# A decoder block on one Trainium2 core: first loads ahead of the semaphore counts, one buffer fill moved, and 40 matmuls whose results nobody reads

## The reference

```python
nx = _ln(x, ln1_scale, ln1_bias)
q, k, v = heads(nx @ W_qkv)
x = x + attend(q, k, v, causal) @ W_self_out
nx = _ln(x, ln2_scale, ln2_bias)
q = heads(nx @ W_q)
k, v = heads(encoder_output @ W_kv)
x = x + attend(q, k, v, None) @ W_cross_out
nx = _ln(x, ln3_scale, ln3_bias)
return x + relu(nx @ W1 + b1) @ W2 + b2
```

## Time and profile before

| | us |
|---|---|
| median of 3 runs | 992.72 |
| lowest and highest | 990.99, 992.97 |
| the profiled execution, its own time | 988.45 |
| its span, first to last instruction | 986.7 |
| PE busy (share of the span) | 958.7 (97%) |
| VectorE busy | 742.7 (75%) |
| ScalarE busy | 639.8 (65%) |
| GpSimd busy | 257.2 (26%) |

### The profile page before, as it was taken

The page is one execution under the profiler, slowest core; times in us unless marked ns, Lnnn a source line. Parts: engine busy times, 40 slices in busy tenths (PEclk is TensorE's granted clock), DMA queues, the critical chain, the costliest instruction groups (busy, mean ns, idle before and its releaser), DMA issues.

```text
span 986.7 us, 20078 instructions
## 1 busy us (share of the span) xinstructions
PE 958.7 (97%) x7632; PEld 599.0 (61%) x7632; DVE 742.7 (75%) x1175; ACT 639.8 (65%) x1371; POOL 257.2 (26%) x451
## 2 busy tenths in 40 slices
PE   4999999999999999999999999999999999999998
PEld 3876665445545555445443764444444699999997
DVE  7579779999999999999923787888887844455542
ACT  4653357777778787777777324888888644444543
POOL 6522123333222223232244210111114312222210
PEclk9999999999999999999999998999999999999999
DMA  6996762232323131313525887334441111122001
GB/s 210 316 352 230 247 195 90 80 99 68 110 67 109 56 100 59 102 52 104 173 90 169 270 318 234 99 124 145 139 130 36 64 55 54 65 65 64 23 21 43
DMA packets 78272, 124.01 MB, mean 126 GB/s; under 512 B 10624, under 2 KB 51872, under 8 KB 73120
## 3 DMA queue, kind: packets, MB, share of 16 engines
q1 hardware_dynamic: 78176, 122.73, 38.1%
HBM read 72.48 MB, written 49.17 MB: 123 GB/s over the span
## 4 chain that ended last, share of the span: by engine, by line
PE 89%; DVE 7%; ACT 1%; DMA 1%; SPq 1%; issue 1%; POOL 0%; ACTq 0%; DVEq 0%
PE bank L862 20%; PE bank L841 17%; PE bank L717 12%; PE bank L698 10%; PE bank L699 9%; PE bank L700 9%; DVE mx L1222 6%; PE bank L896 3%; PE bank L690 3%; PE bank L725 2%; PE bank L685 2%; DMA xt<-in_x_dram 1%; PE bank L738 1%; ACT probs L1115 1%; DVE probs L1215 1%
## 5 line engine op out<-in xcount | busy, mean ns | idle before, releaser
L1115 ACT ACTIVATE probs<-bank 128x512 f32<-128x512 f32 (+3 forms) x1024 | 456.8, 520 | 113.7 <-PE bank L841 107.1
L1222 DVE TENSOR_REDUCE mx<-bank 128x2 f32<-128x1024 f32 (+5 forms) x416 | 435.6, 1084 | 32.8 <-PE bank L717 19.9
L841 PE MATMUL bank<-q_st,k_st 64*128 64x512 f32 (+3 forms) x1024 | 265.9, 425 | 4.8 <-ACT probs L1115 3.5
L862 PE MATMUL bank<-probs,nx_mem 128*32 128x512 f32 (+3 forms) x2048 | 230.8, 528 | 0.4 <-POOL probs L1583 0.4
L841 PEld LDWEIGHTS bank<-q_st,k_st 64*128 64x128 f32 x1024 | 131.4, 186 | 154.4 <-ACT probs L1115 138.8
L717 PE MATMUL bank<-k_st,q_st 62*128 62x154 f32 (+4 forms) x1280 | 217.8, 352 | 4.8 <-DVE mx L1222 2.1
L717 PEld LDWEIGHTS bank<-k_st,q_st 62*128 62x128 f32 x1280 | 131.0, 188 | 71.9 <-DVE mx L1222 54.9
L1583 POOL TENSOR_SCALAR_AFFINE_SELECT probs<-probs 128x256 f32<-128x256 f32 x256 | 103.7, 409 | 198.4 <-ACT probs L1115 196.2
L1592 POOL TENSOR_TENSOR oN<-oT,rs 128x256 f32<-128x256 f32 x64 | 40.6, 635 | 212.8 <-DVE rs L1326 212.8
L1153 ACT ACTIVATE hT<-bank,b_sb 128x512 f32<-128x512 f32 x64 | 44.2, 690 | 72.7 <-PE bank L700 72.7
L1474 DVE TENSOR_TENSOR hT_lo<-hT,hT_hi 128x512 fp32r<-128x512 f32 x64 | 42.7, 687 | 54.5 <-ACT hT_hi L1156 53.5
(11 more groups left out here) (126 smaller groups left out, 1263.7 us busy)
## 6 DMA issues: line engine op xcount, KB each, us to landing
q_st<-q_parts SPq DMA_DIRECT2D x48, 256.0 KB
q_st<-qx_parts SPq DMA_DIRECT2D x48, 256.0 KB
xt<-in_x_dram SPq DMA_DIRECT2D x16, 512.0 KB, 5.9
q_parts<-probs SPq DMA_DIRECT2D x16, 512.0 KB, 4.4
k_parts<-probs SPq DMA_DIRECT2D x16, 512.0 KB, 3.9
k_st<-k_parts SPq DMA_DIRECT2D x32, 256.0 KB
qx_parts<-probs SPq DMA_DIRECT2D x16, 512.0 KB, 4.8
v_aug<-vst_mem SPq DMA_DIRECT2D x8, 544.0 KB, 4.4
```

What stands on the lines that cost most here:

```text
L841: pe.matmul(bank[:, score_bank(a, use), 0:n], keys_of(a, v0)[rows, i // 2, P * kb:P * kb + P], q_st[w][rows, i // 2, lo:lo + n], start=Tru ...
L862: last = pe.matmul(bank[32 * i:32 * i + 32, acc_bank(a, v0, hf), lo - HF * hf:lo - HF * hf + n], v_cur[w // 2][:, col:col + 32], probs[:, ...
L1115: act.activation(probs[:, use % NPT, 0:n], bank[:, score_bank(a, use), 0:n], ACT.Exp, scale=SCALE).then_inc(a.exp_done, 1)
L1222: dve.tensor_reduce(mx[:, par, part].rearrange("p (j y) -> p j y", j=2)[:, :, blocks.start:blocks[-1] + 1:blocks.step], banks[:, :, 0:len( ...
```

## The change

Four edits.

1. SP issues the first loads (x, `wqkv`, the vectors, second x, `wkv`, `cx`) first and raises the 13 semaphores after them, ahead of `b2` and the three late weights.
2. VectorE's fill of `k_st[0]` moves from the start of its program to after the second normalization; that of `q_st[0]` stays. The counts that SP and ScalarE wait for follow (6 instead of 7 where the fill of `k_st[0]` isn't needed, 7 ahead of the first `load_stacks`).
3. At the beginning TensorE makes 18 fp32 matmuls of 128x128 by 128x128 of `ident` into bank 7 as soon as `ident` is there, and 8 more after the first transposes.
4. In the last self span it makes 3 fp32r matmuls (128x128 by 128x256, from pair 3 of the stacks, into the unused half of bank 5) at the end of step 13 and 3 at the end of step 14. In the halves 6 and 7 of `dense_c` it makes 4 (128x128 by 128x512, from `k_st[0]`, into bank 0) after the two tiles and ahead of the wait for `nxT`; the wait for `lo_ready` ahead of them is the one that stood before the first projection. Nobody reads what these 40 write.

```diff
-        def fill_stacks(eng, w, filled):
-            eng.memset(q_st[w][:, :, :].rearrange("p i t -> p (i t)").bitcast(F32), 0.0).then_inc(filled, 1)
-            eng.memset(k_st[w][:, :, :].rearrange("p i t -> p (i t)").bitcast(F32), 1.0).then_inc(filled, 1)
+        def fill_stacks(eng, w, filled, sides=(0, 1)):
+            for side in sides:
+                eng.memset((q_st, k_st)[side][w][:, :, :].rearrange("p i t -> p (i t)").bitcast(F32), float(side)).then_inc(filled, 1)
 ...
-            for s in range(8):
-                sp.sem_inc(A.parts_stored[s], 16)
-            for s in range(2):
-                sp.sem_inc(v_stored[s], 16)
-                sp.sem_inc(px_stored[s], 16)
-            sp.sem_inc(vx_stored, 16)
             load_x(A, x, 0, 0)
 ...
             load_ctx(0)
+            for s in range(8):
+                sp.sem_inc(A.parts_stored[s], 16)
+            for s in range(2):
+                sp.sem_inc(v_stored[s], 16)
+                sp.sem_inc(px_stored[s], 16)
+            sp.sem_inc(vx_stored, 16)
             sp.dma_start(b2_sb[:, :], b2.partition_broadcast(P)).then_inc(w_late, 16)
 ...
+            def keep_busy(dst, a, b, times):
+                for _ in range(times):
+                    pe.matmul(dst, a, b, start=True, stop=True)
+
             pe.wait_ge(consts_ok, 1)
+            keep_busy(bank[:, 7, 0:P], ident[:, :], ident[:, :], 18)
 ...
             transposes(A, 0, 0, 0)
+            keep_busy(bank[:, 7, 0:P], ident[:, :], ident[:, :], 8)
 ...
                 if step % 2 and step < 16:
                     project_c(0, step // 8, step // 4 % 2, (step // 2 % 2,))
+                if step in (13, 14):
+                    keep_busy(bank[:, 5, D:2 * D], k_st[3][:, 0, 0:P], q_st[3][:, 0, 0:D], 3)
 ...
                         between(i)
+                    if n >= LATE_X:
+                        pe.wait_ge(C.lo_ready, 2 + 2 * n - 1)
+                        keep_busy(bank[:, 0], k_st[0][:, 0, 0:P], k_st[0][:, 0, 0:HF], 4)
                     pe.wait_ge(C.nxT_ready, 2 * n + 2)
 ...
-            fill_stacks(dve, 0, ones_ok)
+            fill_stacks(dve, 0, ones_ok, (0,))
 ...
             normalize(A, xt, 1, 1)
+            fill_stacks(dve, 0, ones_ok, (1,))
             for b in range(B - 3):
                 dense_a(b, True)
```

More of the change, by code:

```diff
@@ L438, in _ @@
                 load_x(A, x, 1, hf)
-            sp.wait_ge(ones_ok, 7)
+            sp.wait_ge(ones_ok, 6)
             for b in range(B - 3):
@@ L486, in first_stacks @@
                         sp.wait_ge(A.parts_stored[s], 16 + 16)
-                    sp.wait_ge(ones_ok, 2)
+                    sp.wait_ge(ones_ok, 7)
                     load_stacks(SA, 0, 0)
@@ L1084, in _ @@
                                scale=lns_sb[:, 0, k:k + 1]).then_inc(nxT_high_a, 1)
-            act.wait_ge(ones_ok, 7)
+            act.wait_ge(ones_ok, 6)
             act.wait_ge(w_in, 16 * 6)
```

## The result

The changed kernel takes 997.33 us (median of 20 runs, 992.23 to 1000.07), the kernel before 990.3 in 20 runs on the same chips (988.09 to 992.97). The ratio is 1.0063, with a 95% interval of 1.005 to 1.0076: slower, by 0.63% or 6.2 us. That is the difference of the two means; the medians are 7.0 us apart. The forecast was +3.6 us.

A forecast was written before the change was run, and what follows sets the result against it. PE was taken to bound the kernel, busy 97% with the chain on it for 89%. Terms +1.0 + 0 + 0.7 + 1.9 + 0 = +3.6 us on 992.72 gave 996.3 us, range 990.5 to 998.8.

The forecast's parts named there:

- What it said would be seen: First load about 0.8, fill 18.5, moments 20.4, PE idle about 2 us, added matmuls without waits, slow stretches still there.
- The loads and the fill: At the beginning, loads free up to 0.8 us but the 1.76 us fill delays PE's third projection: +1.0, bounds -0.8, +1.8.
- The clock: Behind 530 and 609 us, work placed before dense stretches cannot fill the thin stretches behind: 0, bound -2.7.
- The 26 at the beginning: PE's start, where the chain stands on loads and VectorE, so a raised clock brings next to nothing: 0, -0.5 to +1.
- The 6 in the span: Last self span, 6 x 0.12 us between chain pieces without a gap: +0.7, from 0 to +1.4.
- the 8 in the halves: Halves 6 and 7, 4 x 0.235 us each behind the second tile, not hidden: +1.9, from 0 to +2.2.
- The clock was not held: Rival for stretches behind 530 and 609 us: added work prevents both slow stretches, -2.7 against +3.6, 993.6 us; chance 0.20.
- The faster case: Rival, whole change: added matmuls and fill hidden, loads pay fully, clock held, -3.5, 989.2 us; chance 0.13.
- Half hidden: Rival: fill absorbed behind PE, part of the halves' matmuls run while VectorE is late, about +1.8, 994.5 us; chance 0.09.
- the fall behind 530: Last self stretch: the clock falls at 530 after ScalarE sets the pace, taken to agree with idleness lowering it; 0.9 us.

The follow-up runs named there:

- the fill at 27.5 us: Kernel before with the first loads early and the `k_st[0]` fill behind VectorE's fourth `low`, no added matmuls: 991.72 us against 990.97, ratio 1.0005.
- the wait filled: Changed kernel plus seven matmuls of `ident` in PE's wait ahead of the third projection: 995.34 us against 991.91 for the kernel before, ratio 1.0038.
- the last kernel: Kernel before with early loads, fill behind the fourth `low`, 26 beginning matmuls, scores made twice in thin stretches: 987.62 us against 991.91, ratio 0.9957.
- the kernel with doubled scores: Kernel before with scores made once more in two thin stretches, same 64-row shape, plus five matmuls at 133 us: 987.71 us against 991.91, ratio 0.996.
- the five at 133 us: Kernel before with only five matmuls of `ident` ahead of the self attention, where TensorE waits for ScalarE: 992.52 us against 992.13, ratio 1.0008.

## Why the prediction was right, and where it was not

Slower was right, and 997.33 lies in the range of 990.5 to 998.8. The size was too small: +0.63% measured, +0.36% forecast. That the forecast of 996.3 came within 1.0 us is partly luck. It starts from a median of three runs, 992.72, where twenty gave 990.3; from 990.3 the same sum gives 993.9, 3.4 us short. The range ends 6.1 us above the median that it starts from, so a loss of 6.2 us was just beyond the largest that it allowed for. Step by step:

**What it said would be seen.** The first load stands at 0.81 as said. The added matmuls stand in the chain without a gap on either side, and there are slow stretches still. The fill starts at 19.02 and not 18.5, the moments at 20.78 and not 20.4, and PE waits about 2 us ahead of the third projection, as said.

**The loads and the fill, forecast +1.0.** The mechanism is right: the fill lies on the chain at its full length and eats the early loads. The term was 0.2 too small, +1.2, since the working took 0.1 us between normalization and fill and the row of the fill shows an idle time of 0.38 ahead of it even in before. That number was in the earlier trace rows and wasn't used. The experiments agree on the place: with the fill's move the whole costs 6.2 us, without it 2.2 (0.22%); with the early loads alone or with the fill at 27.5 us nothing can be measured.

**The clock, forecast 0: this step failed.** The working said that the change "doesn't touch" the clock after the beginning and weighed only whether the added matmuls *hold* it. The two profiled executions show otherwise: of the 5.7 us between them the work makes +3.9, close to the +3.6 of the sum, and the clock +1.8: +1.5 behind PE's wait at 24 us, +1.3 at 140 and -1.0 at 530. Over all runs, too, the changed kernel's clock is lower: a median of 0.989, where 105 runs of the kernel before, timed beside the experiments, have 0.993.

What that is worth can be estimated from the runs' own figures. A mean clock of 0.993 over a span of 990 us, if the low part is at half, is (1 - 0.993) x 2 x 990 = 14 us of slow clock; 0.989 is 22 us. Over the 105 runs the time goes with it as 986.9 + 0.37 x slow us (correlation 0.83); a slow microsecond costs 0.37 because other engines set the pace in much of it. The 8 us more are 3.0 us, which leaves 3.2 to the work. The 20 runs of the changed kernel give 989.8 + 0.34 x slow us, so at no slow clock the two kernels are 2.9 us apart. These agree with a sum of lengths that was about right and a clock term of some 3 us that was missing. It is an estimate and not a measured split: the 20 runs of before beside the result have no clock on record and a median 1.1 us below that of the 105, and the 26 matmuls alone have a median clock of 0.992 at no loss of time.

Which part of the change lowers the clock is not shown. The wait behind the fill is one candidate: in after and in the kernel with edits 1 and 2 the clock falls right behind it, in the first dense work of the program, and with the fill's move undone that stretch is at 1.00. The 26 matmuls are another. Of the five traces that have them, four show a slow stretch between 11 and 28 us: from 11.9 in the 26 alone, from 18.3 with the wait filled, from 19.8 in the last kernel, from 24.0 in after. Two of these kernels have no wait behind a fill, and one has its slow stretch ahead of the wait. Of the nine traces without the 26, only that of edits 1 and 2 has such a fall.

**The 26 at the beginning, forecast 0.** Right as a median (0.9999). The reason given was wrong in part: it held that PE is at full clock by 19.44 in before too. The nine traces without these matmuls have the second transposes at 1.06 us five times and at 1.94 four times. And the clock matters there: two of the four (the six in the span alone, and the kernel with doubled scores) have the beginning of before unchanged, and are 2.2 and 1.4 us behind its trace at 40 us, where the three others with that beginning are within 0.5 us of it. With the 26 the transposes take 1.06 to 1.09 us in four traces of five. That spares some executions a loss, but the median doesn't show it.

**The 6 in the span, forecast +0.7, and the 8 in the halves, forecast +1.9.** The six make +0.9 (0.35 + 0.55): the price per matmul was taken from a run of equal ones, which holds for the first three (0.35, three times the 0.12 of the earlier trace rows), not for the three behind a weighing (32 columns wide), which take 0.55. The eight take 1.12 and 1.13 us behind the tiles (62 rows) and not 0.94, but the projection behind them gets shorter, and what stays is 0.83 + 0.93 = +1.8: right. Alone, the two edits measure 0.1 and 0.11%, 1.0 and 1.1 us, with intervals that hold zero.

**The rivals.** The clock was not held: matmuls that stand 7 us ahead of a thin stretch did not keep it up in either place. The one thing that might have counted for that rival, the missing stretch at 530 in after, is contradicted by the kernel with the six alone, and is missing without them too. The faster case was to be decided at the first `low`: it is at 22.57, later than 21.35, and the case is dead. Half hidden fell with it.

The Trainium skill ("TensorE: Matmul & The Clock Gate", Part 1) warns that the gate runs freely against the program, so that one kernel shows a different number of slow matmuls each time. This case agrees: with the same beginning, the second transposes take 1.06 us in the traces of before, of the eight in the halves and of the five at 133 us, and 1.94 in those of the six in the span and of the doubled scores. Its advice to keep TensorE busy is borne out where the work stands in the thin stretch in the right shape (0.9957 and 0.996), not where it stands before it. The prediction took the fall behind 530 for such idleness. The profile shows none there: PE is busy for 3.00 of 3.00 us ahead of it. What is thin is the number of matmuls.

**What stays open.** By their ratios the parts taken alone give +2.0 (edits 1 and 2), -0.1, +1.0 and +1.1 us, together 4.0, and the whole gives 6.2. Each has an interval of about 1.7 us either way, so the difference may be chance or an interaction. If there is one, it is between the fill's move and the added matmuls: without the move the whole measures 2.2 us, near the sum of its parts. The fill's move together with the 26 alone was not run, nor the fill's move without the early loads. Nor is it settled where the changed kernel's extra slow clock lies in its slower runs: a trace shows one execution, and the two groups of the kernel with the filled wait show that executions of one kernel can lie 6 us or more apart.

## What to carry to other kernels

In this kernel, matmuls that nobody reads kept TensorE's clock up only where they stood inside the thin stretch, in the shape of the work around them, and then in most executions; put ahead of it, on a chain that is already on TensorE, they cost their length. When an operation moves to a place where TensorE comes to wait for it, count its length and its start gap on the chain, and then ask what may happen to the clock of the dense work behind. When a load comes earlier, look at which engines now work side by side. Judge a clock question by the granted clock of all runs, never by one trace.

## What the runs showed of the hardware

- **A shape change is dear.** A 128-row matmul of 256 columns between 64-row ones takes 0.31 us and its neighbour 0.42, against 0.26 and 0.23 when both use 64 rows. 28 such matmuls (and five elsewhere that cost nothing alone) made the kernel 23 us slower; the clock stayed at 0.50 for 11 us and for 20 us in which PE counted as fully busy. A busy row doesn't say how many matmuls get through: 30 there in 11 us, 87 in the kernel with the six in the span.
- **The low clock varies by execution.** The kernel before ran at mean clocks of 0.989 to 0.997, and slow stretches at 140 and at 530 come in some traces and not in others. By the fit one slow us costs 0.37 us of time.
- **The row of the granted clock doesn't show the slow start.** It reads 1.00 from 18 to 24 us in the kernel with the six in the span, while transposes take 1.94 us there that take 1.06 at full clock.
- **Doubled scores hold it, mostly.** 12 and 16 of them in two thin stretches brought the mean clock from 0.993 to 1.000 in seven of nine runs and took 4 us off in the median.
- **VectorE and GpSimd slow each other.** Beside GpSimd's subtractions of 0.72 us two of VectorE's, of 128 x 64, took 0.76 us each, where they take 0.22 in before.
- **A fill has a start gap.** The 0.38 us ahead of VectorE's fill of `k_st`, 128 x 2048, is there wherever it is put: at 3.44, 19.02, 20.36 and 27.53 us.
- **Raising a semaphore on SP takes time.** 13 of them ahead of the first load are 1.59 - 0.81 = 0.78 us, 0.06 us each.
